# GpSimd's indirect stores set apart, a new order of the first loads and of a group's products, in a fused graph layer and mixture of experts

## The reference

```python
def _L0_gnn_ref(x, adjacency, epsilon, W1, b1, rms_weight, W2, b2):
    neighbor_sum = jnp.einsum('bnm,bmd->bnd', adjacency, x)
    agg = epsilon * x + neighbor_sum
    h = jnp.einsum('bnd,dh->bnh', agg, W1) + b1
    h = jax.nn.silu(_rmsnorm(h, rms_weight))
    return jnp.einsum('bnh,hd->bnd', h, W2) + b2

def _L0_ffn_ref(x, gamma, beta, Wr, br, W1, b1, W2, b2):
    xn = (x - mu) * jax.lax.rsqrt(var + EPS) * gamma + beta
    logits = jnp.einsum('bsd,de->bse', xn, Wr) + br
    top_vals, top_idx = jax.lax.top_k(logits, K)          # K = 2 of E = 8
    w = jax.nn.softmax(top_vals, axis=-1)
    ...
    for e in range(E):
        h = jax.nn.gelu(jnp.einsum('bsd,dh->bsh', xn, W1[e]) + b1[e], approximate=False)
        y_e = jnp.einsum('bsh,hd->bsd', h, W2[e]) + b2[e]
        y = y + y_e * w_full[..., e, None]
    return y

x = x + _L0_gnn_ref(_layernorm(x), adj, ...)
x = x + _L0_ffn_ref(_layernorm(x), ...)
```

## Time and profile before

| | us |
|---|---|
| median of 3 runs | 462.79 (462.18 to 462.91) |
| the profiled execution | 462.02 |
| its span, first to last instruction | 460.2 |

### The profile page before, as it was taken

How to read it: one execution, slowest core, us unless ns; L and a number is a source line. 1 busy time by engine, 2 the same in 40 slices (tenths; PEclk the granted TensorE clock), 3 DMA queues, 4 the chain that set the end, 5 groups by cost and what they waited for, 6 DMA issues and landing times.

```text
span 460.2 us, 11870 instructions
## 1 busy us (share of the span) xinstructions
PE 404.1 (88%) x2894; PEld 346.2 (75%) x2894; DVE 306.8 (67%) x1303; ACT 280.3 (61%) x645; POOL 247.4 (54%) x315
## 2 busy tenths in 40 slices
PE   1999999999999999998739487999999999999970
PEld 0557877877777777776729486999999889999970
DVE  4596777889887777768544393666666766656540
ACT  1278776778777777787637253766666666444520
POOL 1123546676667777766642544465556555545450
PEclk9999999999999999999967887999999999999995
DMA  6679773223233221111253223555554433433110
GB/s 206 180 228 309 249 232 92 85 95 114 95 105 115 86 80 46 41 47 38 77 146 86 91 89 95 146 147 154 139 131 127 137 107 107 114 101 105 36 43 6
DMA packets 40890, 53.24 MB, mean 116 GB/s; under 512 B 5812, under 2 KB 35636, under 8 KB 40183
## 3 DMA queue, kind: packets, MB, share of 16 engines
q1 hardware_dynamic: 33040, 32.95, 25.9%
q0 software_dynamic: 6096, 18.52, 11.9%
q10 hardware_dynamic: 1686, 1.01, 0.8%
HBM read 37.75 MB, written 22.31 MB: 131 GB/s over the span
## 4 chain that ended last, share of the span: by engine, by line
PE 56%; DVE 11%; issue 10%; DVEq 9%; ACT 4%; another core or an unknown queue 3%; POOL 2%; DMA 2%; ACTq 0%; POOLq 0%
PE banks L576 10%; PE banks L599 9%; PE banks L737 9%; PE banks L724 9%; PE banks L564 6%; PE banks L585 5%; PE banks L621 3%; DVEq L1417 2%; DVEq L1434 2%; PE banks L611 2%; DVE acc L1417 2%; DMA rms_bc<-rms_w 2%; DVE result L1442 1%; DVEq L1442 1%
## 5 line engine op out<-in xcount | busy, mean ns | idle before, releaser
L526 POOL DMA_INDIRECT out<-result,rows_in x92 | 89.8, 976 | 81.9 <-DVE result L1442 68.1
L737 PE MATMUL banks<-w_sb,hidden_e 128*128 (+1 forms) x736 | 102.3, 283 | 4.8 <-DVE result L1442 2.5
L737 PEld LDWEIGHTS banks<-w_sb,hidden_e 128*128 128x128 f32 x736 | 92.5, 196 | 7.9 <-issue 7.3
L877 ACT ACTIVATE hidden_e<-banks 128x512 f32<-128x512 f32 x92 | 55.0, 598 | 56.3 <-PE banks L724 30.7
L489 POOL DMA_INDIRECT rows_dram<-rows_out,row_of x64 | 66.6, 1040 | 25.2 <-issue 14.7
L599 PE MATMUL banks<-gw_sb,hidden_t 128*128 128x128 f32 x512 | 68.8, 277 | 0.0
L576 PE MATMUL banks<-gw_sb,agg 128*128 128x512 f32 x128 | 66.3, 603 | 0.8 <-ACT agg L812 0.8
L599 PEld LDWEIGHTS banks<-gw_sb,hidden_t 128*128 128x128 f32 x512 | 63.5, 192 | 0.8
L1428 DVE SCALAR_TENSOR_TENSOR acc<-banks,rows_in,acc 128x128 f32<-128x128 f32 x92 | 32.2, 350 | 46.7 <-PE banks L737 25.0
L797 ACT ACTIVATE hidden<-hidden,rrms 128x512 f32<-128x512 f32 x64 | 45.7, 715 | 18.0 <-POOL rrms L466 18.0
L990 DVE TENSOR_TENSOR hidden<-banks,rms_bc 128x512 f32<-128x512 f32 x64 | 43.9, 687 | 12.2 <-ACT hidden L789 12.2
(11 more groups left out here) (141 smaller groups left out, 708.1 us busy)
## 6 DMA issues: line engine op xcount, KB each, us to landing
rows_in<-rows_dram SPq DMA_DIRECT2D x92, 132.5 KB
adj<-adj_t SPq DMA_DIRECT2D x16, 512.0 KB, 3.9
x_tok<-x SPq DMA_DIRECT2D x16, 256.0 KB, 3.9
rows_dram<-idle_in POOLq DMA_DIRECT2D x1, 3710.0 KB
rows_dram<-idle_in SPq DMA_DIRECT2D x28, 132.5 KB
out<-result,rows_in POOLq DMA_INDIRECT x92
w_sb<-w SPq DMA_DIRECT2D x1, 1024.0 KB, 6.3
b_bc<-b SPq DMA_DIRECT2D x1, 1024.0 KB, 11.5
```

The costliest lines, as they stand in the source:

```text
L526: nc.gpsimd.indirect_dma_start(out=out, out_offset=bass.IndirectOffsetOnAxis(ap=rows_in[:, i % RING][:, IDX_AT:IDX_AT + 1].bitcast(U32), a ...
L737: last = pe.matmul(y_ps(i)[:, w], hidden_e[:, i % 4, w * HCE + c], w2_sb[:, bass.ds(at + c * D, D)], start=(c == 0), stop=(c == HCE - 1))
L877: nc.scalar.activation(hidden_e[:, i % 4], h_ps(i), ACT.Gelu).then_inc(gelu_done, 1)
```

## The change

1. *GpSimd in the graph steps.* The four stores of a group are sent one at a time. A new `leave_space` writes a scratch tile (`space`, 128x128) with a memset; it and the token copy `put_tokens` stand between stores 0 and 1, and store 1 comes ahead of `scale2`. `rms` is split in halves of two tiles, one ahead of the last store and one behind it, and silu of tiles 0 and 1 waits for the first half alone.
2. *GpSimd at the turn and in the tile stage.* A copy of high weights or a memset stands between most stores. The even tiles below 20 get their high weights from GpSimd, too (`high_by_gpsimd`). From tile 20 on, odd steps make a memset, and results that are behind are sent one more in every fourth step. The ring of loaded tiles has 20 slots.
3. *First loads.* The identity is loaded alone; the other constants come later. The first adjacency, W1, its bias (now broadcast to all rows) and the RMS weights are issued when the first tokens are there. `sum_weights` stands behind the first `aggregate`; a new `mix_gw1` adds the bias on VectorE, and `fold_gw1` moves to step 1, `prep_rank` to step 3.
4. *A group's products.* `turn_to_features` comes behind `turn_hidden(g3, 3)` and `narrow(g3, 2)`, `router` behind `narrow(g3, 3)`. ScalarE keeps the last turned tile ahead of the expert input.

```diff
-RING, SENDS = 16, 12
+RING, SENDS = 20, 12
...
+        gw1_raw, gb1_bc = hidden[:, HR - 1], hidden[:, HR - 2]
...
         def high_by_gpsimd(i):
-            return EARLY <= i < NT and i % 2 == 0
+            return i < NT and i % 2 == 0
...
+                if g == 0:
+                    sp.wait_ge(x_in[0], 16)
                 if g == 1:
                     sp.wait_ge(adj_in[0], 16)
                 sp.dma_start(adj[:, g % AR], adj_view[g]).then_inc(adj_in[g % AR], 16)
...
-            def rms(g):
-                pool.wait_ge(sumsq_ready, TPG * (g + 1))
+            def rms(g, half):
+                tiles = slice(2 * half, 2 * half + 2)
+                pool.wait_ge(sumsq_ready, TPG * g + 2 * half + 2)
...
+            def leave_space():
+                n = next(spaces)
+                if n > 1:
+                    pool.wait_ge(spaced, n - 1)
+                nc.gpsimd.memset(space[:], 0.0).then_inc(spaced, 1)

             for s in range(STEPS):
                 if g6 is not None:
-                    send_rows(g6, (0,))
+                    send_rows(g6, 0)
+                if g4 is not None:
+                    put_tokens(g4)
+                if g6 is not None:
+                    leave_space()
+                    send_rows(g6, 1)
                 if g4 is not None:
                     scale2(g4)
-                    put_tokens(g4)
                 if g0 is not None:
                     scale1(g0)
                 if g5 is not None:
                     shares(g5)
                 if g6 is not None:
-                    send_rows(g6, (1, 2, 3))
+                    send_rows(g6, 2)
                 if g2 is not None:
-                    rms(g2)
+                    rms(g2, 0)
+                if g6 is not None:
+                    send_rows(g6, 3)
+                if g2 is not None:
+                    rms(g2, 1)
...
-            send_rows(NG - 3, (0, 1))
+            send_rows(NG - 3, 0)
+            pool.wait_ge(table_ready, 2)
+            place_high(0)
+            send_rows(NG - 3, 1)
+            place_high(2)
+            send_rows(NG - 3, 2)
+            leave_space()
+            send_rows(NG - 3, 3)
             scale2(NG - 1)
             put_tokens(NG - 1)
-            send_rows(NG - 3, (2, 3))
             shares(NG - 2)
-            send_rows(NG - 2, (0, 1, 2, 3))
...
+            place_high(4)
+            send_rows(NG - 2, 0)
+            place_high(6)
+            send_rows(NG - 2, 1)
+            leave_space()
+            send_rows(NG - 2, 2)
+            leave_space()
+            send_rows(NG - 2, 3)
+            place_high(8)
+            send_result(0)
+            leave_space()
+            send_result(1)
+            shares(NG - 1)
+            place_high(10)
+            send_result(2)
+            leave_space()
+            send_result(3)
+            place_high(12)
+            send_rows(NG - 1, 0)
+            place_high(14)
+            send_rows(NG - 1, 1)
+            leave_space()
+            send_rows(NG - 1, 2)
+            place_high(16)
+            send_rows(NG - 1, 3)
+            leave_space()
+            send_result(4)
+            place_high(18)
+            sent = 5
+            for i in range(sent, sent + 4):
                 send_result(i)
+                leave_space()
+            sent += 4
             pool.wait_ge(table_ready, 4)
             for step in range(EARLY, TILES + SUM_LAG + 1):
-                if (i := tile_at(step, 0)) is not None and high_by_gpsimd(i):
-                    place_high(i)
-                if (i := tile_at(step, SUM_LAG + 1)) is not None:
-                    send_result(i)
+                if high_by_gpsimd(step):
+                    place_high(step)
+                else:
+                    leave_space()
+                while sent <= min(step - SUM_LAG - 1, TILES - 1):
+                    send_result(sent)
+                    sent += 1
+                    if step % 4 != 3 or sent > step - SUM_LAG - 1:
+                        break
+                    leave_space()
...
             def sum_weights():
-                pe.wait_ge(wide_in, WIDE)
+                pe.wait_ge(gw1_in, 16)
                 pe.wait_ge(parts_made, 1)
-                pe.matmul(hid_ps[:, 2], minus_part[:], gw1_sb[:], start=True, stop=False)
-                pe.matmul(hid_ps[:, 2], row_part[:], gb1_row[:], start=False, stop=True).then_inc(sums_done, 1)
+                pe.matmul(hid_ps[:, 2], minus_part[:], gw1_raw, start=True, stop=True).then_inc(sums_done, 1)
...
-            sum_weights()
...
+                if s == 1:
+                    sum_weights()
...
-                if g4 is not None:
-                    turn_to_features(g4)
                 if g3 is not None:
                     turn_hidden(g3, 3)
                     narrow(g3, 2)
                 if g4 is not None:
-                    router(g4)
+                    turn_to_features(g4)
                 if g3 is not None:
                     narrow(g3, 3)
+                if g4 is not None:
+                    router(g4)
...
+            act.wait_ge(x_in[0], 16)
+            act.dma_start(gw1_raw, gw1).then_inc(gw1_in, 16)
+            act.dma_start(gb1_bc, gb1.partition_broadcast(P)).then_inc(gb1_in, 16)
+            act.dma_start(rms_bc[:], rms_w.partition_broadcast(P)).then_inc(wide_in, 16)
...
-                if t == 0:
-                    act.wait_ge(rrms_ready, g + 1)
+                if t % 2 == 0:
+                    act.wait_ge(rrms_ready, 2 * g + t // 2 + 1)
...
+            def mix_gw1():
+                dve.wait_ge(gw1_in, 16)
+                dve.wait_ge(gb1_in, 16)
+                nc.vector.scalar_tensor_tensor(gw1_sb[:], gb1_bc, 1.0 / (D * SHIFT), gw1_raw, ALU.mult, ALU.add
+                                               ).then_inc(gw1_mixed, 1)
+
             def fold_gw1():
                 dve.wait_ge(sums_done, 1)
+                dve.wait_ge(gw1_mixed, 1)
                 nc.vector.tensor_tensor(gw1_sb[:], hid_ps[:, 2], gw1_sb[:], ALU.add).then_inc(gw1_ready, 1)
+                dve.wait_ge(wide_in, 16)
```

More of the change, by code:

```diff
@@ L1 @@
+import itertools
 from contextlib import ExitStack
@@ L270, in build @@
         sums_done = sem("sums_done")
+        gw1_mixed = sem("gw1_mixed")
         gw1_ready = sem("gw1_ready")
+        spaced = sem("spaced")
         router_cols = sem("router_cols")
@@ L487, in send_rows @@
                     pool.wait_ge(rows_ready, g + 1)
[L488 to L493 removed]
+                nc.gpsimd.indirect_dma_start(
+                    out=rows_dram,
+                    out_offset=bass.IndirectOffsetOnAxis(ap=row_of[:, g * TPG + t:g * TPG + t + 1], axis=0),
+                    in_=rows_out[:, g % RO, t], in_offset=None
+                ).then_inc(rows_sent[g % RO], 16)
+            spaces = itertools.count(1)
+            def leave_space():
[3 more added lines that the diff above has]
+                nc.gpsimd.memset(space[:], 0.0).then_inc(spaced, 1)
             for s in range(STEPS):
@@ L538, in _ @@
-            for i in range(3):
-                send_result(i)
-            shares(NG - 1)
-            for i in range(3, 6):
-                send_result(i)
-            send_rows(NG - 1, (0, 1, 2, 3))
-            for i in range(6, EARLY - SUM_LAG - 1):
-                send_result(i)
+            place_high(4)
[6 more added lines that the diff above has]
+            send_rows(NG - 2, 3)
@@ L552, in _ @@
+            while sent < TILES:
+                leave_space()
+                send_result(sent)
+                sent += 1
             for k in range(SENDS):
@@ L1193, in _ @@
                     prep_bias()
+                    prep_rank()
                     prep_router(0)
```

54 lines of the change are left out of this document (22 added, 32 removed).

## The result

| | before | after |
|---|---|---|
| median, 20 runs each | 463.43 (461.9 to 467.54) | 461.15 (458.82 to 463.33) |
| the profiled execution | 462.02 | 460.8 |
| its span | 460.2 | 459.0 |

The ratio is 0.9934, with a 95% interval of 0.9916 to 0.9952: 2 to 4 us faster, where 16 were forecast, and outside the range of 442.5 to 459. TensorE is busy 400.6 us (404.1 before), ScalarE 275.1 (280.3), GpSimd 282.8 (247.4).

The account below looks back on a forecast made before the run. The prediction took TensorE's products to bound the kernel, so only gaps could be won. From 462.0 us, -14.3 - 3.4 + 0.5 + 1.5 = -15.7 gave 446.3, or 447 as a median, with a range of 442.5 to 459.

Parts of the forecast that it names:

- The reading of the holds: While GpSimd's stores follow closely, TensorE's signals to other engines are held, and are let go after the run.
- Item 1: Turn from groups to tiles: copies or memsets between stores shrink runs to three at most and end the holding, -14.3 us.
- The second and third: Holds at the turn beside seven stores each, from 250.65 and from 272.20: priced at -6.3 with -1.9 for the clock, and -4.0.
- Item 2: Graph stage, TensorE's order: transposes to features moved later cover waits of 0.16 us a step and 1.2 in the last, -3.4.
- the first hold: At the turn, beside five stores from 226.11 to 232.24: logits read at 231.1 instead of 233.26, -2.1 us.
- Item 3: Graph stage, GpSimd: added memset and halved RMS steps fit in its idle time, 0 us, from 0 to +3.
- the rival of a GpSimd that becomes the bound: Graph stage: GpSimd's idle time overfilled or `scale2` late, 7 us on top, 454; 0.27 together with holds only partly ended.
- Item 4: First loads: first aggregation starts sooner, but VectorE's queue gives the gain back, 0 us, from -1.5 to +1.2.
- Item 5: Tile stage, GpSimd: ten more copies, and six leftover results caught up one more in every four steps, +0.5 us.
- Item 6: What stays held at the turn beside the new, still dense series of stores: +1.5 us, from 0 to the whole 14.3.
- Longer runs hold longer: Rival: a hold ends when the series ends, whatever stands between, so pauses lengthen it by 5.6 us, 465; chance 0.09.
- Not the stores: Rival: something else at the turn, such as tile loads or fills, makes the holds, and they remain, 460; chance 0.14.

Follow-up runs that it names:

- again: The kernel before, unchanged, run on another chip, one without holds: 447.62 us (one run).
- spread5: The changed kernel with the backlog of results sent two at a time, not all at once, on a chip that holds: 460.5 us, 0.9927 of before.
- series: The kernel before with extra series of 4 to 10 constant stores, bare or parted by memsets or powers, in five graph steps: 507.4 us (one run), before 463.8.
- turn: The kernel before with the change's turn and tile stage alone, on a chip that holds: 465.11 us, 1.0032 of before.
- pair2: The kernel before with the change's graph stage and first loads, turn and tile stage as before, on a chip that holds: 456.58 us, 0.9846 of before.
- changed: The changed kernel, unchanged, on a chip without holds: 441.29 us beside 448.34, ratio 0.984.
- order: The kernel before with the change's TensorE and ScalarE order in the graph stage alone, on a chip without holds: 444.57 us beside 449.32, 0.9889.
- the graph part: The kernel before with the change's graph stage alone (GpSimd's order and halves, TensorE's and ScalarE's order), on a chip that holds: 456.94 us, 0.9876 of before.

## Why the prediction was wrong, point by point

**The reading of the holds: their size right, their conditions not.** Item 1 priced the holds at 14.3 us, 2.1, 8.2 and 4.0. `again`, which has none, is ahead by 3.1 at tile 3, by 6.6 more at tile 9 and 4.5 more at tile 17: 14.2. That they go with GpSimd's series of stores is borne out by spread5 and the changed kernel, where they moved with the series. That a series is all it takes is not: eight bare stores of `series` held nothing, and on four chips no series did. Nor is everything held until the series ends: ScalarE is let go at 254.16 (after 1.22 us) and at 275.94 (after 2.48) in the middle of two series of before, and at 226.29 in the changed kernel. What else it takes isn't settled. The row loads are not it: the kernel before issues none between 244.48 and 258.68, and from 250 to 258, in which most of the second hold lies, 0.61 MB move on the queue of GpSimd's DMAs and none on that of the loads. What else the turn has and a graph step hasn't (where the stores go, what waits beside them) no run varied.

**Item 1, -14.3: measured +1.5** alone (`turn`, 1.0032), and 4 us more than the list of before when the other parts are there too (0.9934 against the 0.9846 of `pair2`). The step that failed is "the runs of the earlier trace rows shrink to three at most". It counts a memset or a copy as an end of a run, for which no row of before spoke, and the rows after it show that it isn't: in the first series 4.5 us of holds in two results, not 3.1 in one, for a gain forecast of 2.1. The second and third did shrink, from tile 8 to 9 and from 14 to 17, by 3.4 and 6.3 in the changed kernel where 8.2 and 4.0 were forecast, and 1.7 of the 3.4 are gone again at tile 11. But the stores have to go somewhere, and the order made room there by leaving results for later: results 5 to 8, four stores with memsets ahead of the tile loop, stand where the changed kernel loses 3.5 between tiles 17 and 20 (`again` and `changed` lose nothing there).

**Item 2, -3.4: right in size.** Tile 0 of `order` is 3.9 us earlier, its ratio is -3.5 to -6.5 us. Where a step gains it gains 0.32 and not the 0.16 that I read from one wait, four steps gain nothing, and the 1.2 of the last step adds little. On the chip that holds, the graph part gave 5.6 in all at the last tile of its trace: 2.7 at tile 0, where the turned features are now held (ScalarE waits 2.23 us for them), then 2.1 more by tile 3, since the series at the turn ends before the logits are wanted. That is the first hold's 2.1, won by another part than the one I booked it under.

**Item 3, 0: right** as far as it shows; the 1.0 that may be its gain is within the spread. From 160 to 200 in the changed kernel the memset takes 0.22 us (0.25 taken), a half power more than half of a whole one:

```profile
L474 POOL TENSOR_TENSOR rrms<-meansq,minus_half 128x2 f32<-128x2 f32 x7 | 5.1, 732 | 0.5
L509 POOL MEMSET space<- 128x128 f32 x3 | 0.6, 215 | 0.0
```

GpSimd is busy 32.8 of those 40 us (29.15 before) and no engine waits longer for it, so the rival of a GpSimd that becomes the bound is out.

**Item 4, 0: too small.** Alone 0.9921, 2.4 to 5.0 us by its interval; 1.5 at the last tile of its trace. In the changed kernel:

```profile
10.62 3.75 PE L628 MATMUL banks<-adj,xn 128*128 128x256 f32 x8 [10.62 <-DVE xn L1047]
14.16 1.91 PE L708 MATMUL banks<-hidden,minus_part 128*128 128x512 f32 x2
16.95 1.10 PE L640 MATMUL banks<-gw_sb,agg 128*128 128x512 f32 x2 [0.88 <-DVE gw_sb L979]
18.55 1.99 PE L628 MATMUL banks<-adj,xn 128*128 128x256 f32 x8 [0.51 <-DVE xn L1047]
```

The aggregation was forecast at 11.3 and came at 10.62, the end of the sums at 17.1 and came at 16.1, the second aggregation at 19.8 and came at 18.55. Each step was right in kind; I rounded the start up by 0.7 and the sums' end by 1.0, and the second aggregation keeps 1.2 of it.

**Item 5, +0.5: measured +7.4** from tile 20 to tile 25 (7.7 in `turn`), with the misread loop as the step that failed. The ten more copies cost VectorE little: it is busy 306.2 us, 306.8 before. The lockout of which the Trainium skill speaks (SBUF — State Buffer, Who interferes with whom) does not appear in that number, but single rows of the changed kernel agree with it:

```profile
266.85 0.97 DVE L1202 TENSOR_TENSOR upto_p<-upto_sb,full 128x784 f32<-128x784 f32 x1
```
```profile
266.92 1.16 POOL L546 COPY w_high<-w_sb 128x256 f32 x1
```

A copy that takes 0.39 to 0.53 everywhere else takes 1.16 beside a product of two SBUF inputs that began just before it, and in the kernel before a weighted sum that takes 0.35 (line 1434) takes 0.71 at 295.90 beside the copy of 296.04. So the prediction's "no row shows one locked out" holds for its own rows only.

**Item 6, +1.5 for what stays held:** its range went to the whole 14.3, and that end was the true one.

**The rivals.** "Longer runs hold longer" (0.09) came nearest: a memset or a copy doesn't part the stores. It priced the turn at +5.6, and `turn` has +4.8 at its last tile (+1.3 by its median); that the numbers are so close is partly luck, since it has no shrinking second and third hold and no series at step 23. Its 465 missed since the graph stage and the loads brought more. "Not the stores" (0.14) gave 460, next to the 461.15 measured, but by a mechanism in which the turn's order changes nothing, and it moved tile 17 by 6 to 8 us: luck again. I had weighed a series by its bare length, and so gave the two cases in which the pauses win nothing 0.23 together. On a chip that holds nothing the change gives 7 us, less than half of the gain forecast, and all of it from items 2 to 4.

## What to carry to other kernels

A series need not be broken by an instruction that only keeps its engine busy: before pricing such a pause, find in the trace a place of the same stage, with a reader waiting beside it, where one does break it. Stores that are put off to make room come back as a denser series, so follow the backlog to where it is sent, loop condition by loop condition. A wait that the profile can't name may not be a property of the kernel: profile the same kernel on a second chip before planning a change around it, and prefer the edits that win in both. And the idle time of a reader is not the length of a hold: set the time at which it reads against the time at which the result was done.

## What the runs showed of the hardware

- One kernel, two levels of time by chip: medians of 463.4, 463.8 and 464.3 us on three occasions, 447.9 to 449.3 on four. The difference is the held signals. Where they come from (the chip, its host, what runs beside it) is open.
- On a chip that holds: beside three stores 1.36 us apart in the tile stage a reader of TensorE's results waits 2.6 us, beside six 3.0, beside three bare ones at 395.78 2.0. While there are copies between the stores and the results come evenly (tiles 35 to 60) there is no such wait, and eight stores in a row in the graph stage make none. In the kernel before, products done at 253.53 are read at 260.74, 7.2 us later.
- The granted clock was 0.71 and 0.81 in the stretches with the holds and their idle time, 0.83 and 0.93 in the same stretches of `again`. A 128x2 power on GpSimd takes 0.73 us, a 128x4 one 1.04.
